# Layer 1 of a two-layer network: query heads before condition scores, one softmax group finished before the other, half of the weight turns a chunk later

## The reference

```
x = x + attention(condition(x, cond))
x = x + feed_forward(causal_conv(x, cond))      # the conv taps are the condition vectors
```

```
condition:    y = rms_norm(x) * (1 + scale) + shift; q, k, v = y @ W_qkv (16 heads of 16)
              o = softmax(q k^T / 4) v;  out = o + o @ W_out
attention:    layer norm; q = y @ Wq (16 heads of 128), one shared k and v (128); rotary on q, k
              causal softmax;  out = concat(heads) @ Wo          (2048 x 256)
feed_forward: relu(y @ fc.T)^2 @ proj.T, hidden width 1024; fc and proj are quantised to 5 bits
              and dequantised by the kernel itself, in layer 0's time
```

## Time and profile before

| | us |
|---|---|
| median of 3 runs (lowest, highest) | 1414.39 (1413.69, 1414.55) |
| the profiled execution's own time | 1415.49 |
| its span in the trace | 1413.7 |
| TensorE busy | 1301.9 (92%) |
| VectorE busy | 1132.6 (80%) |
| ScalarE busy | 783.0 (55%) |
| GpSimd busy | 142.0 (10%) |

### The profile page before, as it was taken

One profiled execution on the slowest core, in us unless ns is written; L12 is line 12 of the kernel. 1 busy time (PEld: TensorE's weight loads), 2 busy tenths in 40 slices (PEclk: granted clock), 3 DMA queues, 4 the chain that ended last, 5 costly groups with the idle time before them and its releaser, 6 DMA issues.

```text
span 1413.7 us, 25061 instructions
## 1 busy us (share of the span) xinstructions
PE 1301.9 (92%) x9490; PEld 931.3 (66%) x9490; DVE 1132.6 (80%) x2892; ACT 783.0 (55%) x1486; POOL 142.0 (10%) x153
## 2 busy tenths in 40 slices
PE   5999999879799999999999848898999999999988
PEld 2444444558677878777787635575777777686867
DVE  4899999778869686877868888668898888888775
ACT  4999889854465565656565463535353534444213
POOL 0000000111010101010102000010202111110100
PEclk9999999989999999999999979898999999999999
DMA  9333233530111110102030320000000000000000
GB/s 379 113 69 75 68 94 84 151 99 31 38 38 46 31 46 31 46 31 73 5 123 19 148 75 1 23 16 8 9 23 1 23 1 23 1 16 9 8 1 23
DMA packets 26533, 74.18 MB, mean 52 GB/s; under 512 B 3992, under 2 KB 5156, under 8 KB 25136
## 3 DMA queue, kind: packets, MB, share of 16 engines
q1 hardware_dynamic: 25840, 71.62, 16.3%
q10 hardware_dynamic: 576, 0.98, 0.2%
HBM read 49.52 MB, written 23.07 MB: 51 GB/s over the span
## 4 chain that ended last, share of the span: by engine, by line
PE 62%; DVE 30%; ACT 5%; issue 3%; DMA 1%; SPq 0%; ACTq 0%; DVEq 0%
PE psum L616 12%; PE psum L966 8%; PE psum L937 7%; PE psum L725 6%; DVE work L1818 4%; PE psum L664 4%; DVE ffn_mem L1935 4%; PE psum L980 3%; DVE work L1949 3%; PE psum L1005 3%; PE psum L883 2%; PE psum L629 2%; PE psum L674 2%; PE psum L960 1%; PE psum L650 1%
## 5 line engine op out<-in xcount | busy, mean ns | idle before, releaser
L616 PE MATMUL psum<-h_all,w_big 128*128 128x256 f32 x1024 | 243.5, 386 | 11.1 <-ACT work L1269 11.1
L616 PEld LDWEIGHTS psum<-h_all,w_big 128*128 128x128 f32 x1024 | 189.9, 192 | 49.8 <-issue 13.5
L1818 DVE SCALAR_TENSOR_TENSOR work<-work,taps 128x248 f32<-128x248 f32 (+30 forms) x558 | 149.5, 347 | 0.0
L570 PE MATMUL psum<-w_big,h_all 128*64 128x512 f32 x512 | 124.0, 606 | 0.0
L937 PE MATMUL psum<-work,w_big 128*128 128x256 f32 x512 | 120.7, 383 | 0.5 <-DVE gru_mem L2355 0.5
L725 PE MATMUL psum<-w_big,gru_mem 128*128 128x256 f32 x512 | 113.6, 379 | 0.5 <-ACT gru_mem L1311 0.5
L966 PE MATMUL psum<-w_big 128*128 128x256 f32 x448 | 107.3, 391 | 0.0
L937 PEld LDWEIGHTS psum<-work,w_big 128*128 128x128 f32 x512 | 96.1, 191 | 16.0 <-DVE gru_mem L2355 3.3
L725 PEld LDWEIGHTS psum<-w_big,gru_mem 128*128 128x128 f32 x512 | 96.9, 190 | 14.7 <-ACT gru_mem L1311 0.6
L966 PEld LDWEIGHTS psum<-w_big 128*128 128x128 f32 x448 | 85.1, 194 | 19.5 <-issue 7.7
L2353 DVE TENSOR_TENSOR gru_mem<-psum,trig 128x256 f32<-128x256 f32 x128 | 53.8, 421 | 47.6 <-PE psum L937 44.6
(11 more groups left out here) (325 smaller groups left out, 2580.9 us busy)
## 6 DMA issues: line engine op xcount, KB each, us to landing
value_rows<-w_emb SPq DMA_DIRECT2D x128, 128.0 KB, 2.3
work<-value_rows SPq DMA_DIRECT2D x16, 1024.0 KB, 5.8
w_big<-in_Wq SPq DMA_DIRECT2D x2, 2048.0 KB, 16.8
w_big<-in_Wo SPq DMA_DIRECT2D x2, 2048.0 KB, 21.7
out<-w_big SPq DMA_DIRECT2D x15, 256.0 KB, 2.0
x_res<-out SPq DMA_DIRECT2D x15, 256.0 KB, 2.7
w_big<-in_Wv SPq DMA_DIRECT2D x1, 2048.0 KB, 17.8
w_big<-in_Wk SPq DMA_DIRECT2D x1, 2048.0 KB, 23.7
```

Source lines behind the costliest of these rows:

```text
L570: mm = pe.matmul(bank(4 + n)[j * B:(j + 1) * B, :], h_all[:, k, :, 2 * pair + j], w_big[:, 2, k * H * HD + n * 512:k * H * HD + (n + 1) * ...
L616: mm = pe.matmul(bank(n % 2)[:, o * TA:(o + 1) * TA], w_big[:, s, k * H * HD + at:k * H * HD + at + HD], h_all[:, k, bass.ds(i * BA, BA), ...
L1818: ins = dve.scalar_tensor_tensor(dst[:, :, lag:], src[:, :, :T - lag], tap, dst[:, :, lag:], ALU.mult, ALU.add)
```

## The change

TensorE's list, chunks 1 to 6: all of heads 10 to 15 stand ahead of the condition scores of group 0 (before, head 15 stood behind them). In chunk 7 two of the eight `fc` tiles move behind the last heads. `rot_outputs` takes its banks in the order 2, 0, 1, 3 and no longer 2, 3, 0, 1; ahead of its fourth product it waits for `st_on`, which VectorE raises when both groups' scores are out of PSUM. In chunks 1 and 7 half of `rot_project` of group 0 moves ahead of `rot_outputs` of group 1. Only half of the weight pieces (places 0 to 3, which are pieces 4 to 7) are turned in chunk 0; the rest is turned in chunk 1, between the scores and the outputs. `pj` of the last two chunks waits product by product. VectorE and ScalarE get new orders from chunk 1 on; chunk 0 keeps its order.

```diff
+        def o1_bank(n):
+            return bank((2, 0, 1, 3)[n % 4])
+        def piece_at(n):
+            return (n + PIECES // 2) % PIECES
...  TensorE
-                    pe.matmul(bank((2 + n) % 4), v1[rows, g, :], p1_t[rows, g, :], start=True, stop=True)\
+                    if n == 3:
+                        pe.wait_ge(st_on.sem, GA * c + GA)
+                    pe.matmul(o1_bank(n), v1[rows, g, :], p1_t[rows, g, :], start=True, stop=True)\
...  pj: one wait for each product where c >= NA - 2
-                if 0 in groups:
+                ending = isinstance(c, int) and c >= NA - 2
+                if 0 in groups and not ending:
                     pe.wait_ge(h2_on.sem, KF * c + KF)
...
+                        if g == 0 and ending:
+                            pe.wait_ge(h2_on.sem, KF * c + f + 1)
...
-                        if late:
+                        if late and (cond or h < 8):
                             fc(ni - 1, range(h - 2, h))
...
-                        q_heads(i, range(10, 15))
+                        q_heads(i, range(10, H))
+                    if late and rot and not cond:
+                        fc(ni - 1, range(6, KF))
                     if cond:
                         cond_scores(ci, 0)
-                    if rot:
-                        q_heads(i, (15,))
-                    if cond:
                         cond_turn(ci, 1)
                     if rot:
                         rot_scores(i, 0)
                         rot_scores(i, 1)
                     if cond:
                         cond_scores(ci, 1)
+                    if second:
+                        turn_w5(range(PIECES // 2, PIECES))
+                        pe.wait_ge(w5_kept.sem, PIECES)
                     if late:
                         pj(ni - 1, (0,))
                     if rot:
                         rot_outputs(i, 0)
                     if late and cond:
                         pj(ni - 1, (1,))
+                    elif rot:
+                        rot_project(i, 0, range(0, 8))
                     if rot:
                         rot_outputs(i, 1)
+                    if late and cond:
                         rot_project(i, 0, range(0, 8))
...
-                    turn_w5(range(PIECES))
+                    turn_w5(range(PIECES // 2))
...  ScalarE, not begun: cond_exps(0), rot_exps(0), [chunk 1: keep_w5(4..7)], rot_exps(1),
...  keep_rot_outputs(0), spread_cond_probs(0), cond_exps(1), keep_rot_outputs(1), keep_cond_outputs(0)
+                if cond and not begun:
+                    cond_exps(ci, 0)
                 if rot:
                     rot_exps(i, 0)
+                if isinstance(i, int) and i == 1:
+                    keep_w5(range(PIECES // 2, PIECES))
...  (before: rot_exps(0), rot_exps(1), cond_exps(0), keep_rot_outputs(0), spread_cond_probs(0),
...   keep_rot_outputs(1), cond_exps(1), keep_cond_outputs(0))
...  VectorE
-                rlink(dve.transpose(att1.rearrange("p e j -> p (e j)"), bank(2 + g)))
+                dve.transpose(att1.rearrange("p e j -> p (e j)"), bank(2 + g)).then_inc(st_on.sem, 1)
+                dve.wait_ge(st_on.sem, GA * c + g + 1)
...
-                conv2(range(3, 7))
...  (before: conv2(3..6), rot_soft_in(0), rot_soft_in(1), rot_soft_out(0), cond_soft_in(0),
...   rot_soft_out(1), cond_soft_out(0); then conv2 7 to 9 and, behind cond_soft_out(1), 10 to 19)
+                elif rot:
+                    if cond:
+                        cond_soft_in(ci, 0, clink)
+                    conv2(range(3, 4))
+                    rot_soft_in(i, 0, rlink)
+                    conv2(range(4, 5))
+                    rot_soft_out(i, 0, rlink)
+                    rot_soft_in(i, 1, rlink)
+                    conv2(range(5, 6))
+                    rot_soft_out(i, 1, rlink)
+                    if cond:
+                        cond_soft_out(ci, 0, clink)
...
-                    conv2(range(7, 10))
+                    conv2(range(6, 8))
                     cond_soft_out(ci, 1, clink)
-                    conv2(range(10, 20))
+                    conv2(range(8, 20))
```

More of the change, by code:

```diff
@@ L339, in layers @@
                 ("res_on", 1), ("pj_sum", 1), ("y_on", 1)))
-        c_step, r_step = tally("c_step", 26), tally("r_step", 11)
+        c_step, r_step = tally("c_step", 26), tally("r_step", 9)
         block = ctx.enter_context(nc.Block())
@@ L868, in last_chunk, with turn_w5 @@
                 turn_rows(1)
-            def turn_w5(tiles):
-                for n in tiles:
+            def turn_w5(places):
+                for n in places:
                     if n >= 2:
@@ L875, in turn_w5 @@
                     for j in range(4):
-                        mm = pe.transpose(bank(n % 2)[:, j * P:(j + 1) * P], w5_back[n][:, j * P:(j + 1) * P], ident[:])
+                        mm = pe.transpose(bank(n % 2)[:, j * P:(j + 1) * P], w5_back[piece_at(n)][:, j * P:(j + 1) * P],
+                                          ident[:])
                     w5_turned.raised_by(mm)
@@ L1017, in chunk1 @@
                 begun = isinstance(i, int) and i == 0
+                second = isinstance(i, int) and i == 1
                 e = NA - 1
-                if isinstance(i, int) and i == 1:
-                    pe.wait_ge(w5_kept.sem, PIECES)
+                if second:
+                    pe.wait_ge(w5_kept.sem, PIECES // 2)
                 if rot:
@@ L1459, in last_chunk, with keep_w5 @@
                 apply_norm(0)
-            def keep_w5(tiles):
-                for n in tiles:
+            def keep_w5(places):
+                for n in places:
                     act.wait_ge(w5_turned.sem, n + 1)
                     src = bank(n % 2).rearrange("p (j n) -> p j n", j=4)
-                    if n < 4:
-                        dst = fc_t[:, :, 2 * n * P:(2 * n + 2) * P].rearrange("p k (o n) -> p o k n", o=2)
+                    q = piece_at(n)
+                    if q < 4:
+                        dst = fc_t[:, :, 2 * q * P:(2 * q + 2) * P].rearrange("p k (o n) -> p o k n", o=2)
                         src = src.rearrange("p (o k) n -> p o k n", o=2)
                     else:
-                        o, f0 = (n - 4) // 2, 4 * (n % 2)
+                        o, f0 = (q - 4) // 2, 4 * (q % 2)
                         dst = proj_t[:, f0:f0 + 4, o * P:(o + 1) * P]
@@ L1624, in chunk1 @@
                     spread_cond_probs(ci, 0)
+                if cond and not begun:
+                    cond_exps(ci, 1)
                 if rot:
                     keep_rot_outputs(i, 1)
+                if begun:
+                    cond_exps(ci, 1)
                 if cond:
-                    cond_exps(ci, 1)
                     keep_cond_outputs(ci, 0)
@@ L1641, in chunk1 @@
                     row_squares(i + 2)
-                    keep_w5(range(0, 4))
+                    keep_w5(range(PIECES // 2))
                 if prep:
                     scale_rows(i + 2)
-                if begun:
-                    keep_w5(range(4, PIECES))
                 if cond:
@@ L2449, in chunk1 @@
                     add_ffn(e, 0)
-                if cond:
                     cond_soft_in(ci, 0, clink)
-                if rot:
                     rot_soft_out(i, 1, rlink)
-                if cond:
                     cond_soft_out(ci, 0, clink)
-                if begun:
                     add_ffn(e, 1)
+                elif rot:
[10 more added lines that the diff above has]
+                        cond_soft_out(ci, 0, clink)
                 if rot and not cond:
-                    conv2(range(7, T))
+                    conv2(range(6, T))
                     add_attention1(i)
```

12 lines of the change are left out of this document (4 added, 8 removed).

## The result

The changed kernel takes 1400.19 us (median of 4 runs, 1399.26 to 1402.47) where the kernel before takes 1414.47 on the same chip: a ratio of 0.9899, 95% interval 0.9886 to 0.9911. In a second comparison it was 1400.45 against 1414.53, 0.9904 (0.9888 to 0.9921). Faster by 14.3 and 14.1 us, 1.0% each time; the forecast was 13.6 us and 1400.8. The profiled execution took 1399.85 us with a span of 1398.1.

What follows compares the result with a forecast made beforehand. TensorE was taken to bound layer 1. Steady chunks 7.4, end of chunk 0 1.45, chunk 1 2.3, chunk 7 1.3 and tail 1.1 sum to 13.6 us: 1401.9 profiled, 1400.8 median; range 1397.0 to 1405.0.

Steps and rivals of the forecast that it cites:

- TensorE bounds the steady chunks: Layer 1, five steady chunks: only TensorE's idle time can come out, 1.47 us a chunk, 7.4 us in all.
- Head 15: Steady chunks, ahead of the rotary scores: condition scores cover VectorE's last head, the wait goes, 0.6 us a chunk.
- Group 0's probabilities: Steady chunks, ahead of the first outputs: the new softmax order removes the wait, 0.87 us a chunk.
- What is late next: Steady chunks: group 0's probabilities, group 1's and the condition's spreads stay in time, slack 1.1, 0.5 and 0.35 us.
- The added wait: Fourth output product of group 0 waits until group 1's scores are read: costs nothing, at worst 0.3 us a chunk.
- End of chunk 0: Half the turned pieces fall away, but ScalarE's row scaling limits the gain to 1.45 us; TensorE waits 1.5 us.
- Chunk 1: Up to the condition outputs: 3.4 us gained at full clock, 2.3 with one low stretch costing 1.9.
- Chunk 7: Outputs 2.5 us earlier, then 3.3 us idle; gain 3.2 us, or 1.3 with one low stretch.
- Rival 1: Chunks 1 and 7: the clock holds, gains 3.4 and 3.2 us, sum 16.6, total 1397.8 us; chance 0.22.
- Tail: Last two feed-forwards, a wait per product: the first gives 0.1 us, the last 1.0, together 1.1.
- The low clock behind the new waits: Chunks 1 and 7: products behind the new 3.2 and 3.3 us gaps run at half clock, 1.9 us a stretch.
- The transposes: Page's rule that transposes are not busy time speaks against them in chunk 1's gap; chunk 0 does not bear it out.

Runs made afterwards that it cites:

- the stronger form: Changed kernel with the old bank order 2, 3, 0, 1 and the wait for group 1's scores ahead of the second product: one run of 1398.64 us.
- the filler: Changed kernel with six more 128x256 products, into a bank nobody reads, ahead of chunk 7's half projection: one run of 1398.16 us.
- the undoing: Changed kernel with one wait for all eight squared tiles ahead of the last two feed-forward projections: one run of 1401.14 us.
- early rows: Changed kernel with chunk 2's rows scaled between second and third copied piece: 1401.75 us; with chunk 7's copies ahead of the exponential too: 1397.88 us.

## Why the prediction was right

- **TensorE bounds the steady chunks, and nothing but its idle time can come out.** It is busy for all of 64.28 us of a period now. Right, shown.
- **Head 15, 0.6 us a chunk.** 0.53, shown by putting it back. The bound from the modelled overlap (up to 0.68) was needed; the bracket said 0.41.
- **Group 0's probabilities, 0.87 us.** The start of the outputs moved by 0.86 more than that of the scores. But as the price of the softmax order alone this would be wrong: the order is worth 0.35 a chunk beside an early head 15. The sum was right because both edits were replayed together.
- **What is late next: nothing, with slacks of 1.1, 0.5 and 0.35.** Measured 1.0, 0.5 and 0.3. A further 0.10 a chunk came at the condition outputs of group 1 (6.92 us behind those of group 0, now 6.82), where a stall too short to have a bracket went; I had not seen it.
- **The added wait costs nothing.** Shown in the stronger form, two products earlier.
- **End of chunk 0, 1.45 us and a wait of 1.5.** 1.46, and 1.48. Reading ScalarE's list and not counting pieces was the step that mattered.
- **Chunk 1, 2.3 us.** 2.19. The clock fell as assumed, but four terms were off by a little, and partly against each other: the scores came 0.48 earlier and not 0.7, the first outputs 1.83 and not 2.2, the wait ahead of the projection is 2.94 and not 3.2, and the low clock cost 1.7 and not 1.9. The role of the moved pieces for the clock was missed; in the kernel with all pieces in chunk 0 the stretch is 1.74 us longer.
- **Chunk 7, 1.3 us with one slow stretch.** 1.24; the filler prices the slow stretch at 1.64 us (forecast 1.9). The prediction's own numbers give 3.3 and not 3.2 without a slow stretch (1357.15 + 13.8 + 1.07 is 1372.0). Rival 1, the clock holds, would have been this 3.2 or 3.3, and the filler, with 1.24 + 1.64 = 2.9, comes close to it.
- **Tail, 0.1 and 1.0.** 0.12 and 1.07, shown by the undoing.
- **The low clock behind the new waits.** The choice for it was right in all traces with these waits, but no run shows a length of wait from which the clock falls. At the full clock before them, waits of 1.69, 2.08 and 3.13 us (the last ends at 855.17 us of the changed kernel's first trace) were followed by products at 1.00; 1.93, 2.64, 2.94 and 3.10 by products at 0.50, and so was one of 2.20 with 1.57 and eight outputs ahead of it. The same wait can go either way: that of 2.28 us in chunk 0 kept the clock in nine of twelve traces, and one of 1.99 us a little later kept it in the first trace of the changed kernel (eight products in 1.03 us) and lost it in the second (1.80 us, at a clock of 0.50):
```profile
890.91 1.03 PE L701 MATMUL psum<-ffn_mem,w_big 128*128 128x256 bf16 x8 [1.99 <-ACT w_big L1349]
...
891.02 1.80 PE L701 MATMUL psum<-ffn_mem,w_big 128*128 128x256 bf16 x8 [1.99 <-ACT w_big L1349]
```
  The Trainium skill, "TensorE: Matmul & The Clock Gate", "Why this matters for your kernels", has the clock hold for gaps up to some 3 us. The falls behind 1.93, 1.99, 2.28 and 2.64 us disagree; 2.94, 3.10 and 3.13 are too near to tell. Nor did the rule speak clearly for rival 1, whose gaps of 3.2 and 3.3 us are at its edge.
- **The transposes.** The same page, "Part 4: PE-mode transpose", has transposes not count as busy time. This case speaks the other way: in the kernel before, TensorE did nothing but transposes from 921.49 to 927.30 us, with waits of up to 0.62 us between them, at a clock of 1.00. In chunk 1 of the changed kernel 16 of them and the short waits fill the 3.2 us from 958.04 to the outputs, which then take 1.25 us. Without them the outputs, behind 2.64 us of wait, take 2.67, but that is one trace, and with them and 1.93 us of wait they took 1.98.

  What the low clock costs was taken from rows and came out near: 1.9 forecast, 1.6 to 1.7 measured.

One part was luck: the medians differ by 14.3 and 14.1 us where the stages of layer 1 give 13.6. With a start of chunk 0's turned pieces that varies by 3.7 us between traces, an agreement of the totals within 0.6 us proves little; the stage table proves more.

## What to carry to other kernels

Replay all edits of a change together along the three in-order lists, because waits share their gains: the bracket in front of an instruction prices neither of two edits alone. Before filling an engine's idle time ask who is in front of the queue that ends it (here ScalarE's exponential ahead of its copies), and whether the gap is long enough to cost the clock behind it, which here was worth more than half as much again (1.64 us behind a wait of 2.94). Compare stage lengths between fixed instructions, not spans, when gains are a few us.

## What was not expected of the hardware

- Useless work can pay: 2.6 us of products that nobody reads made a stage 1.64 us shorter.
- Transposes kept the clock up: 5.8 us of nothing else, with short waits, ran at 2.4 GHz. With 16 of them in chunk 1's gap and 0.69 us of wait the products behind ran at 2.4 GHz as well (1.25 us for eight); without them, in one trace, at 1.2 GHz (2.67 us).
- The same instruction behind the same wait ran at either clock: behind 2.28 us in chunk 0 nine traces have 2.4 GHz and three 1.2 GHz, and where it was 1.2 the first turned piece came 1.1 to 1.2 us later after it.
- The length of a slow stretch is not fixed by the wait ahead of it: in chunk 1, behind 2.92 to 2.94 us, the 16 products took 5.41 us in six traces and 6.42 in the two with early rows. So 1.35 us gained in chunk 0 came with 1.01 lost 40 us later; whether the edit or the earlier fall of the clock in these two traces did it is open.
